# Output layer normalisation of a three-part decoder layer: chunks 0 to 2 on GpSimd, chunk 3 on VectorE

## What is computed

```python
def _layernorm(x, axis=-1, eps=1e-05):
    m = jnp.mean(x, axis=axis, keepdims=True)
    v = jnp.var(x, axis=axis, keepdims=True)
    return (x - m) / jnp.sqrt(v + eps)
...
x = _layernorm(x + _L0_attn_ref(x, ...), axis=-1)
x = _layernorm(x + _L0_xattn_ref(x, ctx_1024, ctx_1024, ...), axis=-1)
x = _layernorm(x + _L0_ffn_ref(x, ...), axis=-1)
return x
```

## Time and profile before

| what | value |
|---|---|
| time, median of 3 runs | 450.4 us (450.26 to 450.72) |
| time of the profiled execution | 451.89 us |
| its span, first to last instruction | 450.1 us |
| TensorE clock granted over the span, mean | 0.942 |
| PE busy | 378.3 us (84%) |
| DVE busy | 303.4 us (67%) |
| ACT busy | 228.3 us (51%) |
| POOL busy | 80.0 us (18%) |

### The profile page before, as it was taken

How to read it: one execution, slowest core, us unless ns; L and a number is a source line. 1 busy time by engine, 2 the same in 40 slices (tenths; PEclk the granted TensorE clock), 3 DMA queues, 4 the chain that set the end, 5 groups by cost and what they waited for, 6 DMA issues and landing times.

```text
span 450.1 us, 11284 instructions
## 1 busy us (share of the span) xinstructions
PE 378.3 (84%) x4714; PEld 285.1 (63%) x4729; DVE 303.4 (67%) x630; ACT 228.3 (51%) x329; POOL 80.0 (18%) x92
## 2 busy tenths in 40 slices
PE   2556366974789999999999999999998989899992
PEld 1345234763566797767687976776685757566672
DVE  4246984469987679998775889998549476056324
ACT  2343046560069875326877853469944315844330
POOL 8910000020044012011131120003311202411001
PEclk9987559996989999999999999999999999999997
DMA  3261028724101360400112703010200310000100
GB/s 93 73 183 39 4 51 248 202 71 128 28 4 41 108 178 1 128 4 4 39 39 82 214 4 106 4 37 4 75 3 2 100 31 6 1 1 0 25 1 23
DMA packets 29420, 26.87 MB, mean 60 GB/s; under 512 B 12673, under 2 KB 27962, under 8 KB 28602
## 3 DMA queue, kind: packets, MB, share of 16 engines
q1 hardware_dynamic: 26042, 25.86, 20.7%
q10 hardware_dynamic: 3136, 0.27, 0.5%
q0 software_dynamic: 192, 0.03, 0.0%
HBM read 18.38 MB, written 7.35 MB: 57 GB/s over the span
## 4 chain that ended last, share of the span: by engine, by line
PE 54%; DVE 17%; DMA 10%; issue 6%; ACT 5%; SPq 5%; POOL 1%; POOLq 0%; DVEq 0%; ACTq 0%
PE ps_f L725 9%; PE ps_s L547 9%; PE ps_f L714 8%; PE ps_f L573 6%; PE ps_f L581 4%; DMA parts_by_head<-part 3%; PE ps_f L677 3%; PE ps_f L520 3%; DMA QS<-parts_by_head 3%; DVE ST L943 3%; PE ps_s L540 3%; DVE MX L946 3%; PE ps_s L556 2%; PE ps_f L526 2%; PE ps_s L636 2%
## 5 line engine op out<-in xcount | busy, mean ns | idle before, releaser
L547 PE MATMUL ps_s<-QS,KS 125*128 125x128 bf16 (+1 forms) x768 | 79.5, 249 | 11.9 <-DVE ST L943 6.6
L547 PEld LDWEIGHTS ps_s<-QS,KS 125*128 125x128 bf16 (+1 forms) x768 | 65.1, 106 | 34.6 <-DVE ST L943 9.0
L846 ACT ACTIVATE HT<-ps_f,hb 128x512 f32<-128x512 f32 x72 | 48.3, 688 | 74.0 <-PE ps_f L714 44.3
L725 PEld LDWEIGHTS ps_f<-w,HT 128*128 128x128 f32 x576 | 68.8, 192 | 8.1 <-issue 6.0
L725 PE MATMUL ps_f<-w,HT 128*128 128x128 f32 x576 | 72.1, 276 | 0.1
L714 PE MATMUL ps_f<-x2T,w 128*128 128x512 f32 x144 | 70.8, 602 | 1.4 <-DVE acc L1056 1.0
L488 POOL TENSOR_SCALAR_AFFINE_SELECT PC<-PC 128x1024 f32<-128x1024 f32 x32 | 34.8, 1094 | 142.2 <-ACT PC L810 142.2
L1060 DVE SCALAR_TENSOR_TENSOR acc<-ps_f,gw,acc 128x128 f32<-128x128 f32 x128 | 35.7, 341 | 21.8 <-PE ps_f L725 21.5
L810 ACT ACTIVATE PC<-ps_s 128x1024 f32<-128x1024 f32 x32 | 32.2, 1024 | 33.4 <-PE ps_s L547 30.1
L803 ACT ACTIVATE ST<-ST 128x1024 f32<-128x1024 f32 x32 | 33.9, 1061 | 28.0 <-DVE ST L974 27.6
L943 DVE TENSOR_TENSOR ST<-ps_s,ST 128x1024 f32<-128x1024 f32 x32 | 38.6, 1207 | 11.0 <-PE ps_s L547 10.9
(11 more groups left out here) (118 smaller groups left out, 525.2 us busy)
## 6 DMA issues: line engine op xcount, KB each, us to landing
parts_by_head<-part SPq DMA_DIRECT2D x16, 384.0 KB, 2.6
QS<-parts_by_head SPq DMA_DIRECT2D x24, 256.0 KB, 3.8
KS<-parts_by_head SPq DMA_DIRECT2D x24, 256.0 KB, 4.3
xin<-in_x SPq DMA_DIRECT2D x16, 64.0 KB, 2.7
cin<-in_ctx SPq DMA_DIRECT2D x4, 256.0 KB, 5.0
w<-in_L_ffn_rw SPq DMA_DIRECT2D x1, 1024.0 KB
out_x<-acc SPq DMA_DIRECT2D x16, 64.0 KB, 1.8
QS<-MP SPq DMA_DIRECT2D x32, 8.0 KB, 2.1
```

The costliest lines, as they stand in the source:

```text
L547: last = nc.tensor.matmul(ps[:, o:o + S], KS[a][0:kd, c:c + S], queries(a, kd, h, j), start=not masked and j == 0, stop=j == NB - 1, skip_ ...
L725: last = nc.tensor.matmul(ps[:, b * E:(b + 1) * E], HT[n % 2][:, f, b * S:(b + 1) * S], w2[:, e, f, :], start=f == 0, stop=f == NF - 1 and ...
L846: nc.scalar.activation(HT[n % 2][:, f, :], ps[:, :], ACT.Gelu, bias=hb[:, e, f:f + 1]).then_inc(ht_ready, 1)
```

## The change

For chunks 0, 1 and 2 the four instructions of the output normalisation leave DVE and are issued on POOL, right behind the `rstd` that POOL makes. POOL then signals SP for the stores. Chunk 3 stays as it was. Lines behind 496 have a number higher by 7 in the changed kernel.

```diff
@@ -494,6 +494,13 @@
                     nc.gpsimd.tensor_tensor(ve[k][:, :], mv[k][:, :, 1], epst[:, :], ALU.add).then_inc(ve_ready[k], 1)
                     g.wait_ge(ve_ready[k], ch + 1)
                     nc.gpsimd.tensor_tensor(rstd[k][:, :], ve[k][:, :], halfm[:, :], ALU.pow).then_inc(rstd_ready[k], 1)
+                    if what == "fln" and ch < NCH - 1:
+
+                        g.wait_ge(rstd_ready[k], ch + 1)
+                        for b in range(NB):
+                            last = nc.gpsimd.tensor_scalar(acc[:, b, :], acc[:, b, :], mv[k][:, b, 0:1], rstd[k][:, b:b + 1],
+                                                           ALU.subtract, ALU.mult)
+                        last.then_inc(ln_ready[k], 1)
@@ -1063,7 +1070,8 @@
                 elif what == "fln":
                     v.wait_ge(dn_done, (ch + 1) * (NEXP + 1))
                     statistics(2, ch, acc)
-                    normalise(2, ch, acc, acc)
+                    if ch == NCH - 1:
+                        normalise(2, ch, acc, acc)
```

## The result

The changed kernel takes 454.7 us (median of 8 runs, 453.4 to 458.1) where the kernel before, run beside it, takes 450.7 (8 runs, 450.3 to 452.8). The ratio is 1.0091 with a 95% interval of 1.0061 to 1.0120: 4.1 us slower, 2.7 to 5.4. The forecast was 449.7 and no change that can be told, with a range from 448.6 to 451.3. The profiled execution of the changed kernel has a span of 452.9 us against 450.1.

A forecast was written before the change was run, and what follows sets the result against it. It took waits around the output normalisations, chiefly chunk 1's chain to the scores, as the bound; -0.74 at chunk 1 plus 0.05 at chunk 2 made -0.7, so 450.4 - 0.7 = 449.7 us, range 448.6 to 451.3.

The forecast's parts named there:

- the drain of all engines ahead of 3c1: Before chunk 3's scores all engines wait for the queries' parts; time off that chain, up to about 1.3 us, moves everything after.
- the 1290 ns held by line 480: At chunk 1's output one DVE normalisation instruction, median 334 ns, was held by POOL's line 480 through the shared port.
- PE's wait at chunk 2: At chunk 2's output PE waits 1.00 us for DVE's line 1056, which waits for the last store to land.
- Step 1: Price of the new POOL instruction, taken as 0.37 us start to start, so four take 1.48 us against DVE's 1.12.
- p: Price of one new POOL normalisation instruction, start to start; taken as 0.37 us.
- the sum's -0.74: Gain at chunk 1's output: the queries' parts leave at about 353.7 instead of 354.44 us.
- Step 2: Chunk 1's output: the queries' parts leave 0.74 us earlier, with line 926 (933 after) held by POOL's line 480.
- 2.2 - 4p: Gain in us at chunk 1's output while SP's queue binds; a loss at p above 0.55.
- Step 3: Chunk 2's output: cost 0 to 0.2 us, taken as 0.05, since the last store still lands behind an instruction load.
- Step 4: Chunk 0's output: no effect; stores up to 0.4 us later, with the scores that need the following parts far off.
- Step 5: Last chunk unchanged; POOL's instructions behind the moved ones up to 1.5 us late, line 480's result read only far behind.
- the slower one: Rival, chance 0.17: at p of 0.73 or more, late stores cost at chunks 1 and 2; at p = 1.0, +3.1, 453.5.

The follow-up runs named there:

- e9: Kernel before, with GpSimd's residual bias of chunk 3's x1T moved behind the first mask of 3c2; ratio 0.9953, 2.1 us faster.
- e14: Kernel before with two tiles acc used in turn and nothing else; ratio 0.9965.
- e8: Kernel before with two tiles acc, chunk 1's stores behind the queries' parts, and an x1T bias edit that had no effect; ratio 0.9989.
- e12: Changed kernel with GpSimd's normalisation instruction in simpler, incomplete forms in chunks 0 to 2, to read its price; not timed.
- e4: Kernel before with only chunk 2's output normalisation moved to GpSimd; ratio 1.0037, 1.7 us slower.
- e2: Kernel before with only chunk 0's output normalisation moved to GpSimd; ratio 1.0001.
- e1: Changed program with the GpSimd branch taken for no chunk, so the instructions are those of the kernel before; ratio 0.9994.
- e5: Kernel before with chunk 3's x1T bias later in GpSimd's order; the edit did nothing and the instruction ran as before; ratio 0.9996.
- e6: Changed kernel with two tiles acc used in turn; ratio 1.0070 to the kernel before.
- e3: Kernel before with only chunk 1's output normalisation moved to GpSimd; ratio 1.0031, 1.4 us slower.

## Why the prediction was wrong

**What bounds the kernel: right.** The chain at chunk 1's output, the drain of all engines ahead of 3c1, the 1290 ns held by line 480, PE's wait at chunk 2: e9 shows the third and e14 the fourth, each worth more than 0.2% by its middle value (e8, which has the second tile too, shows only 0.1%).

**Step 1, the price: this is the step that failed.** I took p = 0.37 between 0.29 (a select) and 0.46 (a tensor_tensor put onto 128 columns). It measured 0.78 to 0.79, beyond both ends. The two rows were of other kinds of instruction, and I treated their prices as bounds. The row that was farther off, the pow at 1.02, was put aside with an argument about operations; it was the only one beyond the truth. As e12 shows, the second operation and the scalars make 0.25 of the 0.78; the barest tensor_scalar, at 0.53, is already beyond the upper end. With the price went the sign: the sum's -0.74 at chunk 1 turned into a loss.

**Step 2, the gain at chunk 1: the formula held, its input did not.** It gave 2.2 - 4p. With the measured 4p = 3.1 it is a loss of 0.9, and with the 3.50 us that the four really took, a loss of 1.3: the parts left 1.32 us later. VectorE's line 933 was not held by line 480, since with the true price that instruction came after it. The reverse happened: the last of GpSimd's four, started 0.2 us after line 933, lasted 1160 ns instead of 792. The same fourth instruction lasts 1147 to 1167 ns, again just behind the start of that line, in all six traces with chunk 1's whole normalisation on GpSimd, and none of those at chunks 0 and 2 does. The other half of the step, that time off VectorE is worth something here, was right: e9 took 0.94 us off and gained 0.47%.

**Step 3, the cost at chunk 2: sized too small.** With p = 0.78 my own rule (nothing until the four take 2.8 us) gives 0.3 to 0.5 us, and the changed kernel's trace shows 0.6, a slow issue in SP's queue included; e4's trace shows 1.5 with a slower one still. Timed, chunk 2 alone is 1.7 us (0.6 to 2.7). The step counted on one late landing to hide the delay, and that landing is not fixed: with one tile and VectorE the last store of chunk 2 took 2.6 to 3.5 us and PE's wait was between nothing and 1.00 us. Nor did the step see that the issue itself can stretch.

**Step 4, chunk 0: right** (e2). **Step 5: right**; nobody waited for the later bias.

**The rivals.** It went the way of the slower one, GpSimd's price at the store, with a chance of 0.17: the mechanism, both its places and the point from which it decides (p of 0.73) are as written. At p = 0.78 the same lines give about +1.4 us, and the traces show 1.6. The time says 4.1 (2.7 to 5.4). Chunks 1 and 2 alone add up to 3.1 us, which is inside that interval. The 1.6 rests on one trace of the kernel before. From the end of chunk 1's rstd to the end of the program the changed kernel took 101.6 us, and the kernels that are as before behind that point 99.9 (before), 99.4 (e1), 99.7 (e2) and 98.7 (e5): 1.8 to 2.9 us less, 2.2 on the mean. So some 2 us of the 4.1 by the middle values, and perhaps next to nothing, are not in the traces. One candidate is the half clock that cost e6 1.7 us after PE's long wait: the profiled execution of the changed kernel doesn't have it, and of the others nothing is known. A slow issue or landing is another; it stays open. The range should have gone to the slow rival's 453.5; I had left that case out as a whole, and even its end lies below the measured 454.7.

The rule of the Trainium skill ("GPSIMD Engine Reference", section Engine selection) that speaks against the move was right in its advice. Its figures, roughly line rate with one input and about twice as slow with two, were both too mild here: the four took 3.13 us on GpSimd and 1.12 on VectorE, 0.78 and 0.28 us a piece, 2.8 times as slow.

## What to carry to other kernels

An instruction that moves to a slower engine is paid for by whoever stands behind its result, so follow its semaphore into the DMA queue: here the stores stood ahead of an urgent transfer and in the way of a buffer's next use. Putting the urgent transfer first and giving the buffer a second tile turned 0.9% slower into 0.5% faster with the slow instructions still in place. The second tile alone did not (0.7% slower): it brought PE sooner to its next wait, and in e6's trace the granted clock fell behind that longer wait as well. And before moving work off a held-up instruction, look for what holds it: one instruction of GpSimd that nobody was waiting for, moved out of the way, gave 0.5%.

## What the hardware showed that I had not expected

- A tensor_scalar of 128x128 float32 on GpSimd takes 0.53 us in its barest form and 0.78 with two operations and two scalars for each partition, where a select takes 0.29.
- VectorE and GpSimd hold each other up in both directions: VectorE's tensor_scalar waited 0.95 us for a tensor_tensor of GpSimd, and GpSimd's tensor_scalar 0.37 us for a tensor_tensor of VectorE with two inputs in SBUF. The first is shown by moving the instruction (e9), the second by six traces that agree.
- The issue of one store in SyncE's queue took 0.6 to 1.8 us in 17 of 272 cases where 0.44 is usual, each time with an instruction load in flight. The landing of chunk 2's last store took 2.8 to 3.5 us where 1.8 is usual, at the same place of the program in the kernel before and in e1 to e3.
- A transfer of 384 KB that meets an instruction load in its midst landed after 3.97 us instead of 2.62 (e6).
- After TensorE had waited 3.43 us its granted clock fell to 0.50 from 364.9 to 368.3 us, which cost about 1.7 us. This is one trace (e6); in the other sixteen, with shorter waits at the same place, it stayed at 1.00.
